# A Mamba layer and a ternary feed-forward on one core: the state part of y moved in TensorE's order

## The reference

```python
x = _rmsnorm(hidden_states, norm_w)
proj = jnp.einsum('bsd,de->bse', x, in_proj_w)          # z, xBC, dt
xc = jax.lax.conv_general_dilated(xc, conv_w, ...)      # 4 taps in time, then silu
def step(h, inp):
    x_t, B_t, C_t, dA_t, dt_t = inp
    h = dA_t[..., None, None] * h + (dt_t[..., None] * x_t)[..., None] * B_t[:, :, None, :]
    y_t = jnp.einsum('bhpn,bhn->bhp', h, C_t)
    return (h, y_t)
y = y + D * xs;  g = y * _silu(z)                       # then a norm in groups
out = jnp.einsum('bsd,de->bse', g, out_proj_w)
```

## Time and profile before

| | |
|---|---|
| median of 3 runs | 1112.99 us |
| profiled execution: its time | 1109.49 us |
| profiled execution: span of the program's instructions | 1106.7 us |
| time outside the span | 2.8 us |
| busy: PE / DVE / ACT / POOL | 92% / 94% / 86% / 78% |
| TensorE's granted clock, mean over the span | 0.972 (full in the slots' stretch) |

### The profile page before, as it was taken

One profiled execution on the slowest core, in us unless ns is written; L12 is line 12 of the kernel. 1 busy time (PEld: TensorE's weight loads), 2 busy tenths in 40 slices (PEclk: granted clock), 3 DMA queues, 4 the chain that ended last, 5 costly groups with the idle time before them and its releaser, 6 DMA issues. The chain is left out here.

```text
span 1106.7 us, 27543 instructions
## 1 busy us (share of the span) xinstructions
PE 1017.9 (92%) x9598; PEld 799.6 (72%) x9598; DVE 1043.0 (94%) x1977; ACT 951.6 (86%) x2812; POOL 865.3 (78%) x585
## 2 busy tenths in 40 slices
PE   5406899999999999999999999999999999998797
PEld 5404667777777777777777777777777777776796
DVE  5998999999999999999999999999999999988774
ACT  3678999999999999999999999999999999985763
POOL 4241578888888888888888888888888888889575
PEclk9858999999999999999999999999999999999898
DMA  6621000000000000000000000000000000021011
GB/s 152 157 99 54 10 2 2 2 1 2 30 2 2 2 30 2 2 2 30 1 2 2 30 2 1 2 2 30 1 2 2 21 1 2 1 80 49 1 39 38
DMA packets 30425, 24.76 MB, mean 22 GB/s; under 512 B 12304, under 2 KB 23184, under 8 KB 30224
## 3 DMA queue, kind: packets, MB, share of 16 engines
q1 hardware_dynamic: 29712, 22.60, 7.1%
q10 hardware_dynamic: 576, 0.41, 0.2%
HBM read 12.78 MB, written 8.13 MB: 19 GB/s over the span
## 5 line engine op out<-in xcount | busy, mean ns | idle before, releaser
L1224 DVE SCALAR_TENSOR_TENSOR conv<-bank,cw,conv 128x511 f32<-128x511 f32 (+1 forms) x570 | 417.1, 742 | 2.0 <-ACT conv L906 1.6
L668 POOL TENSOR_TENSOR lm<-lm,cbs 128x1024 f32<-128x1024 f32 x128 | 304.2, 2377 | 68.0 <-ACT xw L895 68.0
L1214 DVE TENSOR_TENSOR_SCAN lm<-bank,ident 128x512 f32<-128x512 f32 x256 | 298.7, 1210 | 1.5 <-PE bank L1664 1.5
L940 ACT ACTIVATE xdt<-bank,dt_all 128x64 f32<-128x64 f32 x1024 | 221.2, 324 | 34.9 <-PE bank L1685 34.9
L895 ACT ACTIVATE xw<-xdt,lm 128x64 f32<-128x64 f32 x768 | 198.6, 360 | 0.0
L676 POOL TENSOR_TENSOR ssum<-ssum,sq 128x512 f32<-128x512 f32 x96 | 123.0, 1282 | 92.0 <-ACT sq L955 92.0
L647 POOL TENSOR_TENSOR gated<-gated,gate 128x512 f32<-128x512 f32 x128 | 165.3, 1292 | 13.2 <-DVE gated L1271 13.2
L1643 PE MATMUL bank<-xn_hi,w_hi 128*128 128x512 f32 x320 | 156.1, 488 | 8.8 <-DVE conv L1224 8.8
L658 POOL TENSOR_TENSOR gated<-gated,rbs 128x512 f32<-128x512 f32 x120 | 153.7, 1281 | 0.0
L906 ACT ACTIVATE conv<-bank,cb_bias,cw 128x512 f32<-128x512 f32 x186 | 139.7, 778 | 9.4 <-PE bank L1645 7.3
L1740 PE MATMUL bank<-lm,xdt 128*64 128x128 f32 x2048 | 140.8, 280 | 0.0
(11 more groups left out here) (220 smaller groups left out, 1724.9 us busy)
## 6 DMA issues: line engine op xcount, KB each, us to landing
lm<-in_L_attn_in_proj_w SPq DMA_DIRECT2D x4, 512.0 KB, 5.7
xn_scratch<-chan SPq DMA_DIRECT2D x4, 512.0 KB, 7.4
r_stage<-residual_scratch SPq DMA_DIRECT2D x8, 256.0 KB, 3.0
xn_stage<-xn_scratch SPq DMA_DIRECT2D x7, 256.0 KB, 3.2
x_scratch<-r_stage SPq DMA_DIRECT2D x7, 256.0 KB, 2.0
gate<-in_L_attn_hidden_states SPq DMA_DIRECT2D x2, 512.0 KB, 5.0
cdec<-in_L_attn_hidden_states SPq DMA_DIRECT2D x2, 512.0 KB, 6.3
w_out<-in_L_attn_out_proj_w SPq DMA_DIRECT2D x8, 128.0 KB, 7.0
```

Source lines behind the costliest of these rows:

```text
L668: gp.tensor_tensor(lm[:, mr, :, :], lm[:, mr, :, :], cbs[:, :, :], ALU.mult).then_inc(m_done, 1)
L940: act.activation(xdt[:, r, at:at + HP], misc_of("xt", n)[:, at:at + HP], ACT.Copy, scale=dt_h).then_inc(xdt_done, 1)
L1214: V.tensor_tensor_scan(lm[:, m % R, a, :], bc_bank[(3 * m + a) % 2][:, :], ident4[:, :], 0.0, ALU.mult, ALU.add).then_inc(scanned, 1)
L1224: V.scalar_tensor_tensor(out=conv_of(b, ci)[:, shift:S], in0=tile_bank(b, n, t)[:, 0:S - shift], scalar=cw[:, q, t, KW - 1 - shift:KW - sh ...
```

## The change

On TensorE alone, `y_states` is called right behind `y_within` in all four kinds of slot, and the spreads come behind it. In r3 `out_product` was already behind the first spread and comes behind both y parts now. No instruction is added or taken away, and the other engines' programs are the same.

```diff
@@ r == 0
                     gate_tile()
                     transposes()
                     y_within()
+                    y_states()
                     rows(ssd, 2)
                     rows(ahead, 0)
-                    y_states()
                     cb_products()
```

## The result

The changed kernel took 1123.55 us, the median of 5 runs from 1123.04 to 1126.60; the kernel before took 1112.99 (5 runs, 1106.12 to 1117.78). The ratio is 1.0122, with a 95% interval from 1.0083 to 1.0161: slower by about 1.2%. I had said 1118, so the direction was right and the size about half; the time lies in the range of 1101 to 1135. The profiled execution is the one of 1123.55 us, with a span of 1121.7.

The account below looks back on a forecast made before the run. PE was taken to bound the kernel by a small margin over DVE; its 0.48 us saving a unit is eaten by waits for taps, leaving +0.18, about +0.7 a batch, taken as +6 us: 1118 us median, range 1101 to 1135.

Parts of the forecast that it names:

- PE's order sets the time by a small margin; `pend` starts when PE lets it.: Steady stretch: PE runs a 28.72 us unit without a stop, DVE could do about 28.1; `pend` starts 0.03 behind its spread.
- gate tile behind a tap: List of waits before: the only line where another engine holds PE at length, 27 times of at most 0.2 us.
- The spread comes 0.80 later and the step from `y_within` to `y_states` is 1.03.: On PE, the spread for `pend` moves by one `y_states`, 0.80 us, bounds 0.63 and 0.97.
- Fewer changes between kinds save 0.19 in r1.: PE switches kinds of product less: 0.19 us saved in r2 and in r1, about 0.1 in r3, none in r0.
- The late `pend` stops PE through the taps.: DVE gets `pend` 0.80 us later in r3, r0, r2; taps releasing PE had 0.6 to 0.7 to spare.
- The legs: Unit pieces, tile 5 to 2, 2 to 1, 1 to 5: 6.15, 14.59, 8.16 us, before 5.89, 14.71, 8.12.
- rival B: Each PE hand-over costs more, 0.3 us to resume or extra behind `y_within`: +25 us, 1138; chance 0.22.
- The saving is absorbed entirely: PE's gain of 0.48 us a unit is eaten by waits and a little more: 28.90 against 28.72, +0.18.
- rival A: The late `pend` is absorbed and PE's own 28.24 us a unit counts: -13 us, median 1100; chance 0.15.
- -0.48: PE's saving per unit from fewer changes between kinds of product: 28.72 to 28.24 us for PE alone.
- A batch +0.7, the stretch +5 us.: 4 x 0.18 - 0.05 per batch, slots 15 and 7 treated apart; 6.7 batches in the 775 us stretch.
- The beginning (PE half idle) and the end (feed-forward) I count at nothing, within 1 us.: Outside the steady stretch, at the kernel's start and its feed-forward end: no effect, within 1 us.

Follow-up runs that it names:

- spread-first kernel: Against the kernel before: in all four slots the spread for `pend`, then `y_within`, then `y_states`; 1106.3 us, ratio 0.9941; repeated 1105.5 us, 0.9942.
- r1 alone: Kernel before with `y_states` moved right behind `y_within` in slots r1 only; 1105.8 us, ratio 0.9968.
- the last experiment: Spread for `pend` ahead of both y parts in all slots, and in r0 also the first spread for the next slot; 1102.7 us, 0.9924 of before.
- r3 alone: Kernel before with `y_states` moved right behind `y_within` in slots r3 only; 1125.0 us, ratio 1.0133.
- r2 alone: Kernel before with `y_states` moved right behind `y_within` in slots r2 only; 1117.8 us, ratio 1.0052.
- Three experiments: Kernel before with the moved order in r2, r1 or r0 only; 1117.8, 1105.8 and 1115.6 us, ratios 1.0052, 0.9968 and 1.0028.

## Why the prediction was right or wrong, point by point

- *PE's order sets the time by a small margin; `pend` starts when PE lets it.* Right. It is shown by the pair of the changed kernel and the spread-first kernel: same two parts of y together, only the place of the spread differs, and a batch is 116.43 or 114.33. The reading of the list before was wrong in one place, though. The 27 waits of the "gate tile behind a tap" are the gate tile of r1 and weren't waits for the tap: the tile starts 0.89 us after that tap's end, and 0.17 of a step between kinds of product stands under the tap's name. Nor do four taps release PE, as the description of the kernel before has it, but six: (2, 3) releases tile 3 and (3, 3) the gate tile, both in r1. These two stand in front of `chunk_ends` and have 1.69 and 0.19 us to spare in the changed kernel, so the sum didn't need them.
- *The spread comes 0.80 later and the step from `y_within` to `y_states` is 1.03.* 549.31, 550.33, 551.14: 1.02 and 0.81.
- *Fewer changes between kinds save 0.19 in r1.* Right within 0.01 to 0.04, and paid out where nothing takes it: r1 alone has 14.49 for 14.72 in its leg and 28.52 for 28.72 in the unit, and the last experiment 0.10 for one change.
- *The late `pend` stops PE through the taps.* Right. The legs were forecast at 6.15, 14.59 and 8.16; they are 6.17, 14.58 and 8.21. The load starts 0.06 us behind its tap, which rules out rival B's dear hand-over. I had spoken of near 80 loads released by a tap; the list shows 48, and by the distance from the tap's end it is 99.
- *The saving is absorbed entirely* (against rival A). Right, -0.48 became +0.24 in an ordinary unit. In r3 alone and r2 alone it is a loss outright.
- *A batch +0.7, the stretch +5 us.* Too small: +0.95. The two ordinary units are +0.24 each (forecast 0.18), the unit from slot 15 +0.39 (0.33) and the one from slot 7 +0.09 (-0.02). Slot 15 was right here by luck in part: the forecast put the output rows in as work of DVE alone and left out that PE's output product waits for them. Three experiments missed by that (slot 15's first leg at 6.65, 6.39 and 6.40), and only its new place in r3 kept it out of the changed kernel. Over the six batches it is 5.8 us, over the 7.3 batches from the first slots to the last about 7.
- *"The beginning (PE half idle) and the end (feed-forward) I count at nothing, within 1 us."* This is the step that was wrong, a term put at nothing for a reason that no row showed. That PE is half idle in batch 0 is no cover, the opposite: DVE leads there, with nothing of its own to spare, and each held `pend` is lost time, 0.80 in slot 7 and 0.44 in slot 11. Slot 12 lost another 0.33 or so, and with it came a stretch of low clock that cost about 1.5.
- *The end.* The 4.4 us behind the last batch row aren't due to the order of the slots there: with the changed order at the ends only they are 130.6, as before (130.7), and with the order of before at the ends they are 135.2, as in the changed kernel. They go with the clock. The same stretch in the kernel before, the changed one, and the two profiles of the spread-first kernel:

```profile
976.00:1107.00 131.00, 110.95 (x953) 96.29 (x949) 93.45 (x264) 79.03 (x182) 94.59 (x79) 0.93 0.14 44
```
```profile
986.00:1122.00 136.00, 114.59 (x951) 100.46 (x947) 93.14 (x264) 79.11 (x182) 95.39 (x79) 0.89 0.14 42
```
```profile
966.00:1095.00 129.00, 107.67 (x952) 93.82 (x948) 94.07 (x264) 78.84 (x181) 95.28 (x79) 0.96 0.14 44
```
```profile
966.00:1103.00 137.00, 115.36 (x948) 101.13 (x944) 93.11 (x263) 78.89 (x181) 94.51 (x79) 0.88 0.14 42
```

With a granted clock of 0.96 the tail takes 128.4 us (128.6 in r3 only), with 0.93 it takes 130.7, with 0.89 it takes 135.1, with 0.88 it takes 136.9. The work is the same in all four (PE 948 to 953 records). The last two fences are one kernel, 8.5 us apart by the clock of its tail alone, and before has runs from 1105.7 to 1119.3. So of the measured 10.6 us some 7 are the steady loop, 1.2 to 1.6 the fill, and the rest, about 2, is put down to the clock; for the medians that split is an estimate, since one run of each was profiled. The five runs of the changed kernel lie within 3.6 us of each other, and whether its order makes the longer tail more frequent is open.
- *Chances.* I gave 0.28 to slower by over 1%. The forecast of 0.5% was built from the stretch that I had worked out, and nothing was put in for the one that I hadn't.

## What to carry to other kernels

When two engines are both full, look for the small gaps: here three copies that started 0.03 us behind their producer told that any delay of that product reaches DVE, and the distance from a tap's end to the tile that it releases (0.6 to 0.7 us) told how much of a delay comes back. Then put first on the leading engine what another engine waits for soonest, and group the rest by kind, and ask of every product near the moved ones what else it waits for, also once per batch only; the same grouping that lost 1% with the spread behind it won 0.6 to 0.8% with the spread ahead of it. Do the sum also for the filling stages, where the engine that leads is another one.

## What the runs showed of the hardware

A step between kinds of product on TensorE costs 0.1 to 0.2 us here, and how much depends on the two kinds: the last experiment took one away and got 0.10 in its leg, and r1 moved alone got 0.20 a unit for one. Part of the price can stand one product later: behind `y_states` the output product's first two starts are 0.21 us apart, behind a spread 0.11. The Trainium skill, "TensorEngine Tiling (Array Packing)", Key Properties, says that changing the tiling mode drains TensorE. These rows agree with it; it could not decide the case, because the engine that gained by it was then stopped by another.

VectorE's end released a weight load within 0.05 to 0.08 us (taps 0.05 to 0.06, the output rows 0.07 to 0.08). And the pace of a batch in one profile repeats to 0.02 us from batch to batch in most of these kernels (to 0.06 in the changed one), and the same in two profiles of one kernel (114.33 twice), while whole runs of it differ by up to 12 us, and its two profiles by 8.5 us in the tail: an effect of 0.3 us a batch can be read from one trace, where the intervals from 5 to 10 runs are 5 to 10 us wide.
